# Routed experts and the shared feed-forward of a two-layer transformer block as one stream of steps, and a residual addition at another place

## The reference

```python
diff = jax.nn.relu(a1 - lam[None, :, None, None] * a2)
diff = diff / (jnp.sum(diff, axis=-1, keepdims=True) + 1e-06)
out = jnp.einsum('bhqk,bhkd->bhqd', diff, v)
...
return out @ Wo
```

```python
shared = silu(x @ Wsg) * (x @ Wsu) @ Wsd
shared = shared * jax.nn.sigmoid(x @ Wse)
...
xe = jnp.zeros((E, CAP, h), x.dtype).at[sel, posc].add(x[tok] * valid[:, None])
g = silu(jnp.einsum('ech,ehf->ecf', xe, Wg))
u = jnp.einsum('ech,ehf->ecf', xe, Wu)
ye = jnp.einsum('ecf,efh->ech', g * u, Wd)
y_pair = ye[sel, posc] * (w * valid)[:, None]
out = shared.at[tok].add(y_pair)
```

## Time and profile before

| what | value |
|---|---|
| median of 3 runs | 2958.39 us (2957.83 to 2962.09) |
| the profiled execution | 2956.44 us |
| its span | 2954.3 us |
| TensorE busy | 2577.7 us, 87% |
| VectorE busy | 1724.0 us, 58% |
| ScalarE busy | 1080.1 us, 37% |
| GpSimd busy | 1014.0 us, 34% |
| mean DMA rate | 64 GB/s |

### The profile page before, as it was taken

How to read it: one execution, slowest core, us unless ns; L and a number is a source line. 1 busy time by engine, 2 the same in 40 slices (tenths; PEclk the granted TensorE clock), 3 DMA queues, 4 the chain that set the end, 5 groups by cost and what they waited for, 6 DMA issues and landing times. The chain is left out here.

```text
span 2954.3 us, 35819 instructions
## 1 busy us (share of the span) xinstructions
PE 2577.7 (87%) x12276; PEld 1739.3 (59%) x12276; DVE 1724.0 (58%) x4042; ACT 1080.1 (37%) x2539; POOL 1014.0 (34%) x748
## 2 busy tenths in 40 slices
PE   5889898989599999994689998879998677699998
PEld 2334444434288888882567776657776433387776
DVE  4557676765155555546478887458888311156664
ACT  1125454445233333222156666146666211111211
POOL 2318676767311121100056665034444100123330
PEclk9969999999799999997899999999999898899999
DMA  7361212110200000001121000000000599610001
GB/s 259 125 142 28 56 23 51 22 40 1 100 15 15 14 14 28 0 1 62 36 74 36 22 26 12 15 29 8 8 15 1 194 380 357 204 53 20 15 8 57
DMA packets 158052, 189.41 MB, mean 64 GB/s; under 512 B 51406, under 2 KB 105678, under 8 KB 157504
## 3 DMA queue, kind: packets, MB, share of 16 engines
q1 hardware_dynamic: 131776, 147.43, 16.1%
q10 hardware_dynamic: 14592, 27.27, 2.9%
q0 software_dynamic: 11520, 12.64, 1.3%
HBM read 159.85 MB, written 52.43 MB: 72 GB/s over the span
## 5 line engine op out<-in xcount | busy, mean ns | idle before, releaser
L588 DVE TENSOR_REDUCE mx<-bank 128x1 f32<-128x512 f32 x512 | 326.4, 678 | 125.5 <-PE bank L495 121.4
L435 POOL TENSOR_TENSOR probs<-probs 128x1024 f32<-128x1024 f32 x128 | 301.4, 2375 | 211.9 <-PE bank L518 174.9
L646 ACT ACTIVATE probs<-bank 128x1024 f32<-128x1024 f32 x256 | 250.2, 1022 | 274.3 <-PE bank L508 274.3
L822 POOL TENSOR_TENSOR up_lo<-up_raw,up_hi 128x1024 fp32r<-128x1024 f32 (+1 forms) x28 | 74.9, 2695 | 719.2 <-ACT up_hi L812 719.2
L1450 POOL TENSOR_SCALAR mix<-mix,sm 128x256 f32<-128x256 f32 (+1 forms) x256 | 228.7, 904 | 225.5 <-DVE sm L1347 225.3
L1390 ACT ACTIVATE ms<-ms,sm 128x256 f32<-128x256 f32 (+1 forms) x512 | 247.9, 487 | 133.8 <-DVE sm L1318 130.8
L892 DVE TENSOR_TENSOR hid<-bank,sg 128x512 f32<-128x512 f32 x108 | 74.6, 691 | 317.0 <-ACT sg L842 309.7
L842 ACT ACTIVATE sg<-bank 128x512 f32<-128x512 f32 x108 | 64.6, 598 | 482.1 <-PE bank L768 482.0
L495 PE MATMUL bank<-k_parts,q_parts 96*128 96x512 f32 x512 | 216.9, 475 | 10.1 <-DVE mx L588 4.5
L495 PEld LDWEIGHTS bank<-k_parts,q_parts 96*128 96x128 f32 x512 | 93.8, 195 | 171.4 <-DVE mx L588 139.0
L1318 DVE CUSTOM_DVE_ANT_0 ms<-bank,misc 128x256 f32<-128x256 f32 (+1 forms) x512 | 183.9, 397 | 0.1
(11 more groups left out here) (199 smaller groups left out, 5565.8 us busy)
## 6 DMA issues: line engine op xcount, KB each, us to landing
ewg<-in_L_ffn_Wg_dram SPq DMA_DIRECT2D x32, 704.0 KB, 13.2
ewu<-in_L_ffn_Wu_dram SPq DMA_DIRECT2D x32, 704.0 KB, 15.6
ewd<-in_L_ffn_Wd_dram ACTq DMA_DIRECT2D x32, 512.0 KB, 11.5
q_parts<-qk_dram SPq DMA_DIRECT2D x48, 256.0 KB, 4.4
up_raw<-in_L_ffn_W_dram SPq DMA_DIRECT2D x16, 512.0 KB, 4.5
ewd<-in_L_ffn_Wd_dram ACTq DMA_DIRECT2D x32, 192.0 KB, 14.9
qk_dram<-qk_hi SPq DMA_DIRECT2D x4, 1280.0 KB, 5.2
qk_dram<-qk_lo SPq DMA_DIRECT2D x4, 1280.0 KB, 7.2
```

The source lines that it names most:

```text
L435: pool.tensor_tensor(probs[:, even, half, :], probs[:, even, half, :], probs[:, odd, half, :], ALU.add).then_inc(S["paired"], 1)
L588: dve.reduce_max(mx[:, U % 2, q, h:h + 1], bank[:, h, :], AX.X).then_inc(S["max"], 1)
L646: act.activation(probs[:, s % BUFS, 2 * x:2 * x + 2, :], bank[:, 2 + 2 * x:4 + 2 * x, :], ACT.Exp, scale=scale).then_inc(S["exps"], 1)
```

## The change

`experts` and the shared `swiglu` call are replaced by one `feed_forward1`, one block, written out for 44 steps n = 0 to 43. Hidden tile h is n // 4, token chunk c is n % 4. Weights of the shared part are loaded and split one hidden tile at a time, its down rows too, instead of the whole down matrix at the start. The first 16 steps each hold one expert pair too. The pair uses banks 2 and 3 (`A`, `B`) for everything: turned tokens, gate, turned hidden rows in A; up and result in B. The shared ups have banks 0 and 1 alone until step 18, then alternate with 2 and 3. Shared downs no longer add up over two hidden tiles in PSUM: each step adds its four tiles into X, 176 additions. All loads of expert weights, and the copy out of results, are now issued by SP; gate and up weights are two pairs deep, token rows, hidden rows and down weights one. The loads of expert results and their additions to X begin with step 19 and are spread by `halves` up to step 41; they use the room of the expert weights. In `attention1_heads` VectorE's `add(s - 5)` moves from the end of the step to just behind `mask(s, 1)`.

```diff
@@ attention1_heads, @block.vector @@
             if s < UNITS:
                 mask(s, 1)
+            if s >= 5:
+                add(s - 5)
             if 4 <= s < UNITS + 4:
                 values_low(s - 4)
             if s % NT == 4 and s < UNITS:
                 output_low(s // NT)
             if 1 <= s <= UNITS:
                 combine(s - 1)
-            if s >= 5:
-                add(s - 5)
@@ build @@
             attention1(env, r)
-            experts(env)
             feed_forward1(env, r)
@@ Combine and experts removed, feed_forward1 new @@
+    STEPS, PAIRS, FULL = HT * NC, E // 2, (FT1 - 1) * P
+    A, B = 2, 3
+    HALVES, DEPTH, FIRST = 2 * NT, 3, PAIRS + 3
+    got = [sem(f"c_got{m}") for m in range(DEPTH)]
+    ye, slot = env["ye"], r["slot"]
+
+    def ups(n):
+        return 0 if n < PAIRS + 3 or n % 2 == 0 else 2
+
+    def halves(n):
+        return 0 if n < FIRST else min(HALVES, -(-HALVES * (n - FIRST + 1) // (STEPS - 2 - FIRST)))
...
+            @block.sync
+            def _(sp):
...
+                def gate_up(p):
+                    sp.wait_ge(R["up"], CREDIT + p - 1)
...
+                def down(p):
+                    sp.wait_ge(R["y"], CREDIT + p)
...
+                tile(0)
+                tokens(0)
+                gate_up(0)
+                down(0)
+                gate_up(1)
+                for n in range(STEPS):
+                    if 1 <= n < PAIRS:
+                        down(n)
+                    if 1 <= n <= PAIRS:
+                        keep(n - 1)
+                    if n + 1 < PAIRS:
+                        tokens(n + 1)
+                    if n % NC == 0 and n // NC + 1 < HT:
+                        tile(n // NC + 1)
+                    if n + 2 < PAIRS:
+                        gate_up(n + 2)
...
+            @block.tensor
...
+                def up(n, m):
+                    h, c = n // NC, n % NC
+                    if c == 0 and m == 0:
+                        pe.wait_ge(S["split"], CREDIT + 2 * h + 1)
+                    if n == PAIRS + 3:
+                        pe.wait_ge(R["y_s"], CREDIT + PAIRS)
+                    pe.wait_ge(S["hidden" if m else "gated"], CREDIT + (n if n < PAIRS + 3 else n - 1))
...
+                def down(n):
+                    h, c = n // NC, n % NC
+                    if c == 0:
+                        pe.wait_ge(S["split"], CREDIT + 2 * h + 2)
+                    pe.wait_ge(S["parts"], CREDIT + n + 1)
+                    pe.wait_ge(S["added"], CREDIT + SUBS * n)
...
+                def turn_tokens(p):
+                    pe.wait_ge(R["x"], CREDIT + 16 * (p + 1))
+                    pe.wait_ge(R["hT"], CREDIT + p)
...
+                def expert_up(p):
+                    pe.wait_ge(R["xt_s"], CREDIT + p + 1)
+                    pe.wait_ge(R[f"w{p % 2}"], CREDIT + 64 * (p // 2 + 1))
+                    pe.wait_ge(R["y_s"], CREDIT + p)
...
+                for n in range(STEPS):
+                    up(n, 0)
+                    if 1 <= n <= PAIRS:
+                        expert_down(n - 1)
+                    if n < PAIRS:
+                        turn_tokens(n)
+                    up(n, 1)
+                    if n < PAIRS:
+                        expert_up(n)
+                    if n:
+                        down(n - 1)
+                    if n < PAIRS:
+                        turn_hidden(n)
+                down(STEPS - 1)
...
+            @block.scalar
...
+                def high(h):
+                    act.wait_ge(S["raw"], CREDIT + 48 * (h + 1))
+                    act.wait_ge(S["y"], CREDIT + NC * (h - 1))
+                    act.activation(hi[:, h % 2], raw[:, :, :, :], ACT.Copy).then_inc(S["hi"], 1)
+                    act.activation(dh[:, h % 2, :], raw_down[:, :], ACT.Copy).then_inc(S["hi"], 1)
+
+                high(0)
+                for n in range(STEPS):
+                    act.wait_ge(S["up"], CREDIT + 2 * n + 1)
+                    act.wait_ge(S["gated"], CREDIT + n)
+                    act.wait_ge(R["gated"], CREDIT + min(n, PAIRS))
+                    act.activation(sg[:, :], bank[:, ups(n), :], ACT.Sigmoid).then_inc(S["sig"], 1)
+                    if 1 <= n <= PAIRS:
+                        act.wait_ge(R["y"], CREDIT + n)
+                        act.wait_ge(R["stored"], CREDIT + 16 * (n - 1))
+                        act.activation(ys[:, :], bank[:, B, :], ACT.Copy).then_inc(R["y_s"], 1)
+                    act.wait_ge(S["hidden"], CREDIT + n + 1)
+                    act.wait_ge(S["y"], CREDIT + n - 1)
+                    act.activation(hh[:, n % 2, :], hid[:, :], ACT.Copy).then_inc(S["hid_hi"], 1)
+                    if n % NC == 1 and n // NC + 1 < HT:
+                        high(n // NC + 1)
+                    if n < PAIRS:
+                        act.wait_ge(R["up"], CREDIT + n + 1)
+                        act.wait_ge(S["gated"], CREDIT + n + 1)
...
+            @block.gpsimd
...
+                def gather(m):
+                    if m == 0:
+                        pool.wait_ge(R["stored"], CREDIT + 16 * PAIRS)
+                    if m < DEPTH:
+                        pool.wait_ge(R["cleared"], CREDIT + m + 1)
+                    else:
...
+            @block.vector
...
+                def add(n):
+                    dve.wait_ge(S["y"], CREDIT + n + 1)
+                    for s in range(SUBS):
+                        t = n % NC * SUBS + s
+                        dve.wait_ge(S["added"], CREDIT + SUBS * (n - NC) + s + 1)
+                        dve.scalar_tensor_tensor(out=X[:, t, :], in0=bank[:, 4 + s, :], scalar=r["gshared"][:, t:t + 1],
+                                                 in1=X[:, t, :], op0=ALU.mult, op1=ALU.add).then_inc(S["added"], 1)
+
+                def routed(m, n):
+                    t = m // 2
+                    dve.wait_ge(S["added"], CREDIT + SUBS * n)
+                    dve.wait_ge(got[m % DEPTH], 32 * (m // DEPTH + 1))
...
+                for n in range(STEPS):
+                    if n < PAIRS:
+                        dve.wait_ge(R["xt"], CREDIT + n + 1)
+                        dve.wait_ge(R["up"], CREDIT + n)
+                        dve.tensor_copy(xT[:, :, :], bank[:, A, :].rearrange("p (k c) -> p k c", k=KD)).then_inc(
+                            R["xt_s"], 1)
+                    dve.wait_ge(S["sig"], CREDIT + n + 1)
+                    dve.wait_ge(S["hid_hi"], CREDIT + n)
+                    dve.wait_ge(S["parts"], CREDIT + n)
+                    dve.tensor_tensor(hid[:, :], bank[:, ups(n), :], sg[:, :], ALU.mult).then_inc(S["gated"], 1)
+                    dve.wait_ge(S["gated"], CREDIT + n + 1)
+                    dve.wait_ge(S["up"], CREDIT + 2 * n + 2)
+                    dve.tensor_tensor(hid[:, :], bank[:, ups(n) + 1, :], hid[:, :], ALU.mult).then_inc(S["hidden"], 1)
+                    dve.wait_ge(S["hid_hi"], CREDIT + n + 1)
+                    dve.wait_ge(S["y"], CREDIT + n - 1)
+                    dve.tensor_tensor(hl[:, n % 2, :], hid[:, :], hh[:, n % 2, :].bitcast(F32),
+                                      ALU.subtract).then_inc(S["parts"], 1)
+                    if n < PAIRS:
+                        dve.wait_ge(R["sig"], CREDIT + n + 1)
+                        dve.wait_ge(R["turned"], CREDIT + n)
+                        dve.tensor_tensor(ehid[:, 0:F1], bank[:, A, 0:F1], sg[:, 0:F1], ALU.mult).then_inc(R["gated"], 1)
+                        dve.wait_ge(R["gated"], CREDIT + n + 1)
+                        dve.tensor_tensor(ehid[:, 0:F1], bank[:, B, 0:F1], ehid[:, 0:F1], ALU.mult).then_inc(
+                            R["hidden"], 1)
+                    if n:
+                        dve.wait_ge(R["used"], CREDIT + 2 * halves(n - 1))
+                        add(n - 1)
+                    if n == FIRST - 1:
+                        dve.wait_ge(R["up"], CREDIT + PAIRS)
+                        for m in range(DEPTH):
+                            dve.memset(cy[m], 0.0).then_inc(R["cleared"], 1)
+                    for m in range(halves(n - 1), halves(n)):
+                        routed(m, n)
+                dve.wait_ge(R["used"], CREDIT + 2 * HALVES)
+                add(STEPS - 1)
+
```

More of the change, by code:

```diff
@@ L57 @@
     "f1": "raw hi split up sig gated hidden hid_hi parts y added",
-    "e": "w0 w1 w2 d0 d1 x0 x1 xt xt_s up sig gated hidden turned hT y y_s stored padded",
+    "e": "w0 w1 d x xt xt_s up sig gated hidden turned hT y y_s stored padded cleared used out",
 }
@@ L1595, in up @@
-                def up(p):
-                    wait(pe, S["xt_s"], p + 1)
-                    wait(pe, S[f"w{p % DEPTH}"], 64 * (p // DEPTH + 1))
-                    wait(pe, S["hidden"], p - 1)
+                def up(n, m):
[5 more added lines that the diff above has]
+                    pe.wait_ge(S["hidden" if m else "gated"], CREDIT + (n if n < PAIRS + 3 else n - 1))
+                    count = 0
+                    for l, right in PARTS:
+                        for k in range(KD):
```

(19 more changed lines are left out.)

253 lines of the change are left out of this document (95 added, 158 removed).

## The result

| | us, median | lowest to highest |
|---|---|---|
| before | 2959.61 (4 runs) | 2957.83 to 2962.09 |
| changed | 2799.87 (4 runs) | 2798.8 to 2801.1 |

The ratio is 0.9457, with a 95% interval of 0.9443 to 0.9471: 5.4% faster, about 160 us. The forecast was 2828 us with a range of 2808 to 2862, so the direction was right and the time lies 28 us under the forecast and 8 us under the lower end. The profiled execution of the changed kernel took 2798.8 us.

The account below looks back on a forecast made before the run. Routed experts wait for DMA while the neighbouring shared stage leaves DMA idle. From 2956.4 us, merging takes 92.8 and the moved addition 38, giving 2825.6; with 2 us for the median, 2828 us, range 2808 to 2862.

Parts of the forecast that it names:

- The step of 17.11 us: Merged stage, first 16 steps: shared step 8.34 us plus expert pair 8.77, with the 1.64 us expert-up-to-hidden-transposes hand-off hidden.
- rival B: Merged steps: hand-offs show because buffers are single, 1.1 to 3.2 us a pair, 2846 to 2879 us; chance 0.15.
- The start: Merged stage, first load to first matmul: 9.1 us, once instead of twice; unsure by 3 us either way for the transfer.
- The slow first matmuls: Start of merged stage: first 24 matmuls run at the 1.2 GHz level after idleness, 2.6 us lost, now only once.
- One queue for all transfers: Merged steps: SP issues all DMA, some eleven issues and 4 us of 17 a step, holding nothing up: 0 us.
- the floor of 14.9 us: Merged steps: time a step's 5.1 MB of transfers need at 342 GB/s, below which the stage could not go.
- The additions into X: Late steps: VectorE needs 8.0 us against TensorE's 8.34, so 0 us but close; the sum takes 2 us of waits.
- The mutual lock: Steps 19 to 41: VectorE and GpSimd lock each other out, up to 2.3 us at each of five tile loads.
- The addition moved: Layer 1 attention: moving VectorE's addition ahead removes output-projection waits (60, 42.8 us); gain 38 us, bounds 10 and 46.
- C: Attention gives only 10 us, TensorE then waiting for ScalarE's copied weights or VectorE's products: 2856 us; chance 0.15.
- D: Merged steps: one queue instead of two brings weights late, 250 GB/s, 53 us more, 2881 us; chance 0.05.
- E: Merged stage: TensorE's clock falls; under 0.68 mean all gain is lost, 3102 us at 1.2 GHz throughout; chance 0.03.

Follow-up runs that it names:

- the run without cover: Changed kernel with TensorE's shared down moved behind the transposes of the hidden rows: 2822.77 us, ratio 0.9533.
- The packed run: Changed kernel with the 64 routed additions put into 12 steps instead of 23: 2833.94 us, ratio 0.9572.
- the packed runs: Changed kernel with 64 routed additions in 12 steps, 2833.94 us, and the same with GpSimd's gathers ahead of the next tile's low part, 2825.42 us.

## Why the prediction was right or wrong

**What bounds the kernel: right.** A stage that waits for transfers stood beside one that leaves them idle, and merging them gives 94.4 us.

**The step of 17.11 us: right.** 15 of the double steps take 17.17 us. Step 0 pays the hand-off once, as said (1.9 taken, 1.68 waited), and the run without cover shows the price for all 16: 1.70 us a step, within the 1.1 to 3.2 that rival B gave.

**The start: right.** 9.1 us taken, 9.28 measured. Its unsure part, the transfer, did not grow. The slow first matmuls: 24 of them take 5.11 + 2.98 = 8.1 us, 2.5 above the usual 5.60, where 2.6 was taken.

**One queue for all transfers: right.** No wait for weights; 11 issues of about 0.43 us a step. The down matrices land in a median of 5.1 us. The rate of 342 GB/s behind the floor of 14.9 us was read wrongly, as a limit: 395 stands in the trace of before.

**The additions into X: right, with 2 us too many.** None of the 43 other steps waits for them; only the one before the last shared down is left (3.0 us). VectorE is busy 176.46 of 218 us in late steps, 0.81 where I named 0.9: the 8.0 us of a step in the sum held 1 us of waiting for ScalarE, which is not busy time. The mutual lock, which the prediction put at an estimated 11.5 us at most, made VectorE 0.3 to 1.0 us slower at each of the five tile loads, 3.0 us together, and none of it reached TensorE; most of a low part now falls on the sums out of PSUM. The packed run shows that the lock is real when the two meet. That it made the 4.1 us of waits in the old stage was not tested.

**The addition moved: right in its mechanism, mis-sized.** The step that failed is "I take 38 us for both halves; bounds 10 and 46 (42.8 and the slow-clock matmuls after the 1.9 us waits)". It measured 60 us alone and 63.3 in the changed kernel's trace. I took the sum of the wait rows as the most that the addition could cost. But 46 units without such a row waited as well, and those with one waited some 0.2 us longer than it says: TensorE's rows count from the modelled end of the matmul before, and a wait that ends inside that tail leaves no mark. The rows of the weight loads had 66.2 us of idle time against 11.8 in their sister form. "The last two waits of each half remain" did not hold either: of all waits for the addition none is left, and two waits for the low part, 2.2 us, stand in for them.

**The rivals.** B did not come (no wait of the transposes from step 1 on); C did not: TensorE's waits for the weights that ScalarE prepares are 18.4 us in 24 as against 19.3 in 26; D did not; E did not, the clock being granted at 0.98 in the merged stage. None of them had the case that came: a gain larger than the waits shown. The merged stage is 1.6 us under its sum: 2 us of waits did not come and the end is 0.5 us shorter, while 16 double steps are 0.06 us longer each.

## What to carry to other kernels

Before a bound is put on what a moved instruction can give, do not take the sum of TensorE's wait rows for it. A check that needs no wait row: look at when the waiting instruction starts behind the other engine's end. Where that distance is the same to 0.002 us from unit to unit (0.15 us here, in 110 of 126), the unit is bound by it; where it varies (0.16 us and more, 16 units), it is not. The idle time of the weight loads is a hint, when it is set against a sister form on the same line (66.2 against 11.8 us). Against the matmuls it says nothing by itself, since loads idle more than matmuls where nothing waits too. Those of the scores idle as much before (first row) as in the changed kernel (second), while the matmuls of that line idle 0.1 us in both:

```profile
L1249 PEld LDWEIGHTS bank<-k,q 64*128 64x128 f32 x976 | 82.3, 188 | 49.5 <-issue 27.3 <-DVE sm L1318 17.2
L1248 PEld LDWEIGHTS bank<-k,q 64*128 64x128 f32 x976 | 81.4, 186 | 48.8 <-issue 31.1 <-DVE sm L1317 12.8
```

When the whole time is too noisy for a small edit, cut the trace at the stretch that the edit touches: over ten traces attention starts anywhere from 1494.2 to 1502.8 us, but takes 829.7 and 829.8 us in both with the addition at its old place, and 766.4 to 767.2 in the six with it behind the masks.

Two neighbouring stages with opposite limits are worth one stream if each hand-off between them has foreign work of more than its own length behind it; here 2.74 us over 1.64, and without it 23 of the 94 us are lost. When work is packed closer, look first at what stands in the gathering engine's queue ahead of the gathers.

## What was not expected of the hardware

In each of 110 units some 0.2 us of waiting left no mark on the matmul rows. Before the projection, these rows had shown 43.8 us (with three waits of 1.0 us in all that no engine is named for). In all of attention the idle time in them fell by 39.5 of the 63.3 us that went, since 5.2 us of waits are new and 0.9 us of the others gone: 24 us were not to be seen there.

The 16 DMA engines moved 372 GB/s at a share of 1.01 while TensorE kept its step of 17.17 us; 342 GB/s at a mean share of 0.96 had not been the limit.

The last shared down follows 2.97 us of waiting, and TensorE's clock falls just behind the wait, 0.8 us after the matmuls have begun again. The windows before the wait, of the wait, and of the twelve matmuls:

```profile
2776.00:2781.00 5.00, 5.00 (x23) 4.04 (x23) 2.08 (x3) 1.23 (x2) 0.00 (x0) 1.00 0.56 210
2781.20:2784.40 3.20, 0.32 (x2) 0.00 (x0) 2.73 (x4) 0.00 (x0) 0.00 (x0) 1.00 0.00 0
2784.40:2789.10 4.70, 4.57 (x12) 3.32 (x12) 0.00 (x0) 0.00 (x0) 0.00 (x0) 0.64 0.60 223
```

The granted clock is still 1.00 during the wait and 0.64 on average behind it: eight of the twelve matmuls take 0.61 to 0.63 us, at the 1.2 GHz level, where 0.39 is usual. By their starts that costs 1.6 us, on top of the wait. The long waits of the packed runs were followed by slow matmuls too.
